# Moving the second context transpose and the self attention's projection behind the PV of step 5

## The chip, the cores and the metric

One core of one Trainium2 chip runs the whole layer. The metric is the device time of one execution in microseconds (us), lower is better. The kernel is written for each engine by hand: TensorE (PE in the profile, PEld for its weight loads), VectorE (DVE), ScalarE (ACT), GpSimd (POOL) and SyncE (SP, which issues the DMAs). Each engine runs its own list of instructions strictly in program order, and semaphores order the engines against each other.

## The reference, cut to what matters

Eight batch entries of 112 tokens by 256 channels go through one decoder layer:

```
x = LN(x + self_attention(x))            # 16 heads of 16, rotary; heads and batch are swapped before the reshape to (8, 112, 256)
x = LN(x + cross_attention(LN'(x), ctx)) # 16 heads of 64, ctx is 375 x 256 per entry
x = LN(x + moe_ffn(x))                   # 8 experts, top 2, and a shared one
```

Only the first two lines are touched. Because of that swap, two heads of the self attention over all batch entries give the rows of one output entry, and the kernel goes through it in that order. For one entry, self attention ends in a projection (256 to 256) whose sum with x is normalised to x1; x1 is normalised again, transposed and projected to the queries of the cross attention. The keys of the cross attention are `ctx @ w_k`, which needs the context transposed, 256 channels on the partitions in two halves of 128.

## The kernel before, in words

All heavy products are split into a high and a low part (three matmuls for one). After a matmul or a transpose into PSUM, ACT copies the high part to SBUF (`..._hi`) and DVE computes the low part (`..._lo`) as the difference, so nearly every PE result passes through ACT and then DVE before PE may use it.

The attention block runs a software pipeline over the entries b = 0 to 7 (`iterations`, L625: b = 0 unrolled, b = 1 to 6 in a loop, b = 7 unrolled). An iteration has eight steps, s = 0 to 7, one for each pair of cross attention heads. In step s PE does, in this order (L1582 and after): `scores` of pair s; `k_project` of pair s + 2 (in steps 6 and 7 those of pairs 0 and 1 of entry b + 1); now and then a value projection; `p_transpose` of pair s - 1 (the probabilities, six transposes); `pv` of pair s - 2. DVE takes the scores' maxima, ACT the exponentials, POOL the reciprocals and the normalisation of the probabilities.

Between these, the self attention of the next entry b + 1 is laid in pieces, called fills. The table `FILL_AT` (L96) says which fill goes to which place of which step: the key is (step, place), and each of PE, ACT and DVE reads the same table through its own function `place(n)` (L1584, L945, L1236). It is thus an order written out by hand; nothing plans it. Places stand at these points of step 5:

- PE: scores(5), k_project(7), place 1, p_transpose(4), place 3, pv(3), place 4.
- ACT: k_hi(7), place 1, the exponentials of pair 5, place 3, `o_hi`(3), `cpt_hi`(4), place 4.
- DVE: `cpt_lo`(3), the maxima of pair 5, k_lo(7), place 1, place 3, `o_lo`(3), place 4.

Step 6 then begins on DVE with `cpt_lo`(4), `x1_moments` (L1091, which normalises with a reciprocal root from POOL), the maxima of pair 6, `xn_norm` and `k_lo` of the next entry's pair 0; on ACT with k_hi and the exponentials of pair 6; on PE with scores(6), `k_project` of the next entry's pair 0, a value projection, p_transpose(5), the fill NT (transposes of xn) and pv(4).

The fills that matter here are those of step 5 for entry b + 1:

- OT: transposes of the self attention's output rows, which come by DMA; `ot_hi` on ACT, `ot_lo` on DVE.
- C0 and C1: the transposes of the two channel halves of the context, three transposes each; `ctx_hi` (L826) on ACT, `ctx_lo` (L1079) on DVE.
- PJ: the projection, six matmuls (`out_project`, L1433), nothing on ACT, and `residual_moments` (L1084) on DVE: the sum `res`, `bn_stats`, `bn_aggr` and a small add that is the input of POOL's reciprocal root.

The waits that tie them:

```
ctx_transpose(b, 1): pe.wait_ge(sg["ot_lo"], b + 1)                  # C1 after ot_lo
free("PJ"):          pe.wait_ge(sg["ctxt_lo"], 2 * b + 1)            # PJ after ctx_lo of C0
k_project(b, p):     pe.wait_ge(sg["ctxt_lo"], 2 * b + 2)            # after ctx_lo of C1
k_project(b, p):     pe.wait_ge(sg["oct_lo"], PAIRS * b + p - 4)     # for p = 0: after o_lo of pair 3 of the entry before
pv(b, s):            cpt_lo of pair s, kt_lo of k_done, oct_lo of pair s - 1
x1_moments(b):       n1_rstd from POOL, which waits for residual_moments
```

SP loads the next context when both context transposes of an entry are done, and the next residual rows when `res` is done. Entry 0's own self attention stands in a prologue with its own order and does not read the table.

Of the kernel before, what the change touches and what calls it, by code (L numbers as in the profile page):

```python
# [94 lines left out]

FILL_AT = {(0, 2): ["QA"], (0, 3): ["QB"], (0, 4): ["KA"], (1, 0): ["KB"], (1, 3): ["S0", "S1"],  # L96
           (2, 1): ["S2", "S3"], (2, 3): ["T0"], (2, 4): ["T1"], (3, 1): ["O0", "T2"],
           (3, 2): ["T3"], (3, 4): ["O1"], (5, 1): ["OT", "C0"], (5, 3): ["C1", "PJ"],
           (6, 3): ["NT"], (7, 1): ["Q0", "Q1"]}

V_AT = {0: "V02", 2: "V10", 3: "V11", 4: "V12", 6: "V00", 7: "V01"}
# [2208 lines left out]
```

## Time and profile before

| | us |
|---|---|
| time, median of 3 runs | 675.41 (675.35 to 676.03) |
| the profiled execution's own time | 675.51 |
| its span, first to last instruction | 673.7 |
| PE busy | 561.5 (83%) |
| DVE busy | 476.8 (71%) |
| ACT busy | 406.5 (60%) |
| POOL busy | 262.9 (39%) |

The span is what the trace shows; the profiled execution's own time is 1.8 us more, for what lies around it, and stands 0.1 us from the median. Busy shares are means over stages with different limits. The attention block lies between about 88 and 490 us of the span. A row of the timeline gives the start and duration of an instruction (or of several merged ones), and in brackets how long its engine had been idle before it and what released it. Two instructions of ACT or DVE in a row overlap a little in the rows: the distance from start to start is then shorter than the duration. That distance is called a slot below.

### The profile page before, as it was taken

Reading aid. Unit: us, or ns where it says so; the run is one execution under the profiler, and the core shown is the slowest. Engines: PE = TensorE matmul, PEld = TensorE weight load, DVE = VectorE, ACT = ScalarE, POOL = GpSimd, SP = SyncE. Lnnn points to the kernel's source line nnn. Section 1 sums busy time; section 2 is a strip of 40 time slices with the busy share of each in tenths; the row PEclk is TensorE's granted clock in tenths of the full one; section 3 lists DMA queues with packets and bytes.
Section 4 is the critical chain, followed back from the end, with each engine's and each line's share of the span. In section 5 each row is a group of like instructions: output and inputs, shape, how many; then the busy total and the mean of one; then the engine's idle time right before and its main releaser. Section 6 shows DMA issues by size and latency. Waiting matters only on the chain. (4 is left out here: it accounts for less than half of the span.)

```text
span 673.7 us, 14735 instructions
## 1 busy us (share of the span) xinstructions
PE 561.5 (83%) x4972; PEld 387.2 (57%) x4972; DVE 476.8 (71%) x921; ACT 406.5 (60%) x979; POOL 262.9 (39%) x292
## 2 busy tenths in 40 slices
PE   5637677799899899899899899989669877999970
PEld 4526345567566567566566566655554644666640
DVE  1985558888888888888888888877668849533333
ACT  2576457487587587587587587565437728534431
POOL 3431034354354354354354354344415822333331
PEclk9975689999999999999999999999857979999995
DMA  8926201311200200200200200401327777333324
GB/s 242 277 70 192 58 18 32 76 32 34 76 32 31 74 31 31 74 31 31 74 31 31 74 31 31 139 32 61 98 70 246 250 213 208 57 63 57 49 32 117
DMA packets 55330, 57.36 MB, mean 85 GB/s; under 512 B 17286, under 2 KB 44238, under 8 KB 55054
## 3 DMA queue, kind: packets, MB, share of 16 engines
q1 hardware_dynamic: 50910, 50.89, 25.3%
q0 software_dynamic: 4384, 5.99, 5.3%
q8 instruction: 22, 0.36, 0.2%
q14 instruction: 14, 0.11, 0.0%
HBM read 46.74 MB, written 10.13 MB: 84 GB/s over the span
## 5 line engine op out<-in xcount | busy, mean ns | idle before, releaser
L728 POOL TENSOR_TENSOR c_rcp<-c_sum,neg_one 112x2 f32<-112x2 f32 x64 | 44.6, 696 | 191.5 <-ACT probs L882 191.5
L732 POOL TENSOR_TENSOR probs<-probs,c_rcp 112x750 f32<-112x750 f32 x64 | 91.8, 1434 | 5.0
L882 ACT ACTIVATE probs<-ps_s,c_neg 112x375 f32<-112x375 f32 x128 | 72.6, 578 | 26.7 <-DVE c_neg L1128 26.6
L766 ACT ACTIVATE kt_hi<-ps_o 128x376 fp32r<-128x376 f32 x64 | 31.8, 497 | 60.3 <-PE ps_o L159 60.3
L1822 POOL DMA_INDIRECT moe_sum<-gsh_hi,xs_in x21 | 33.2, 1583 | 78.7 <-ACT gsh_hi L1870 62.8
L1132 DVE SCALAR_TENSOR_TENSOR cpt_lo<-ps_t,cpt_hi 125x672 f16<-125x672 f32 x64 | 54.3, 849 | 11.7 <-ACT cpt_hi L889 11.7
L1128 DVE TENSOR_REDUCE c_neg<-ps_s 112x2 f32<-112x750 f32 x64 | 59.4, 929 | 1.3 <-PE ps_s L159 1.3
L2102 PE MATMUL ps_h<-w_ex,xst_hi 128*128 (+1 forms) x168 | 58.5, 390 | 0.9 <-DVE xst_lo L1911 0.9
L1507 PE MATMUL ps_t<-ident,probs 112*128 112x112 f32 x384 | 48.3, 262 | 7.6 <-DVE cpt_lo L1132 7.1
L157 PE MATMUL ps_o<-ctxt_hi,w_k_lo 128*128 128x376 f16 x128 | 42.3, 330 | 12.2 <-DVE oct_lo L1141 11.0
L1507 PEld LDWEIGHTS ps_t<-ident,probs 112*128 112x128 f32 x384 | 40.5, 141 | 17.2 <-issue 9.0
L889 ACT ACTIVATE cpt_hi<-ps_t 125x672 f16<-125x672 f32 x64 | 47.5, 742 | 3.3 <-PE ps_o L1524 3.2
L2028 DVE TENSOR_TENSOR gsh_hi<-ps_g,gsh_hi 128x512 f16<-128x512 f32 x21 | 14.5, 690 | 46.9 <-ACT gsh_hi L1864 46.9
L158 PE MATMUL ps_o<-ctxt_lo,w_k_hi 128*128 128x376 f16 x128 | 42.0, 328 | 0.0
L159 PE MATMUL ps_o<-ctxt_hi,w_k_hi 128*128 128x376 f16 x128 | 42.0, 328 | 0.0
L1123 DVE SCALAR_TENSOR_TENSOR v_lo<-ps_vx,v_hi 125x512 f16<-125x512 f32 x48 | 33.0, 688 | 11.4 <-ACT v_hi L874 11.3
L157 PE MATMUL ps_vx<-w_v_hi,ctxt_lo 128*128 128x512 f16 x96 | 37.3, 388 | 2.6 <-DVE res L1147 1.9
L1008 DVE TENSOR_TENSOR kt_lo<-ps_o,kt_hi 128x376 fp32r<-128x376 f32 x64 | 34.7, 542 | 5.0 <-ACT kt_hi L766 5.0
L1847 ACT ACTIVATE s_act<-ps_h,unscale 128x512 f32<-128x512 f32 (+1 forms) x29 | 19.5, 672 | 30.7 <-PE ps_h L2102 30.1
L804 ACT ACTIVATE work<-ps_a,s_neg 112x112 f32<-112x112 f32 x128 | 33.0, 368 | 8.1 <-DVE s_neg L1043 8.1
L874 ACT ACTIVATE v_hi<-ps_vx 125x512 f16<-125x512 f32 x48 | 28.9, 602 | 14.5 <-PE ps_vx L159 14.1
L1524 PE MATMUL ps_o<-cpt_hi,v_lo 125*64 125x112 f16 x384 | 34.7, 222 | 3.5 <-DVE kt_lo L1008 1.7
(337 smaller groups left out, 1755.6 us busy)
## 6 DMA issues: line engine op xcount, KB each, us to landing
chunk<-in_L_ffn_ew_dram SPq DMA_DIRECT2D x24, 512.0 KB, 3.5
spare<-in_L_ffn_ew_dram SPq DMA_DIRECT2D x18, 512.0 KB, 6.2
store<-in_L_ffn_ew_dram SPq DMA_DIRECT2D x6, 512.0 KB, 6.0
ctx_raw<-in_ctx_dram SPq DMA_DIRECT2D x8, 375.0 KB
moe_in<-chunk SPq DMA_DIRECT2D x1, 2709.0 KB, 13.8
plain_raw<-in_L_xattn_w_kv_dram SPq DMA_DIRECT2D x2, 1024.0 KB, 17.1
xs_in<-moe_in SPq DMA_DIRECT2D x15, 129.0 KB, 2.0
ctx_all<-in_ctx_dram SPq DMA_DIRECT2D x1, 1800.0 KB, 22.7
```

Source lines behind the costliest of these rows:

```text
L157: eng.matmul(out, ll, rh, start=start, stop=False, **kw)
L158: eng.matmul(out, lh, rl, start=False, stop=False, **kw)
L159: return eng.matmul(out, lh, rh, start=False, stop=stop, **kw)
L728: pool.tensor_tensor(c_rcp[:, s % 2, :], c_sum[:, s % 2, :], neg_one[:, :], ALU.pow).then_inc(sg["c_rcp_ready"], 1)
L732: pool.tensor_tensor(p, p, r, ALU.mult).then_inc(sg["p_normed"], 1)
L882: act.activation(probs[:, s % 2, h, 0:SK], ps_s[0:N, h, 0:SK], ACT.Exp, bias=c_neg[:, s % 2, h:h + 1], accum_out=c_sum[:, s % 2, h:h + 1]) ...
L889: act.activation(cpt[0][:, :, :, :].rearrange("p h t n -> p h (t n)"), ps_t[0:SKT, :, 0:ST * N], ACT.Copy, scale=P_SCALE).then_inc(sg["cpt ...
L1008: return dve.tensor_tensor(dst, src, part.bitcast(F32), ALU.subtract)
L1128: dve.tensor_reduce(c_neg[:, s % 2, :], ps_s[0:N, :, 0:SK], X, ALU.max, negate=True).then_inc(sg["c_neg_ready"], 1)
L1132: dve.scalar_tensor_tensor(cpt[1][:, :, :, :].rearrange("p h t n -> p h (t n)"), ps_t[0:SKT, :, 0:ST * N], P_SCALE, cpt[0][:, :, :, :].rea ...
L1507: last = pe.transpose(ps_t[:, h, t * N:(t + 1) * N], probs[:, s % 2, h, t * SKT:t * SKT + P], ident[0:N, 0:N])
L2102: last = pe.matmul(out, lhs[a], rhs[b], start=start and n == 0, stop=stop and n == 2)
```

## The change

One entry of the table moves, and since all three engines read the table, it moves on each of them:

```diff
-           (3, 2): ["T3"], (3, 4): ["O1"], (5, 1): ["OT", "C0"], (5, 3): ["C1", "PJ"],
+           (3, 2): ["T3"], (3, 4): ["O1"], (5, 1): ["OT", "C0"], (5, 4): ["C1", "PJ"],
```

The order in step 5 is then:

- PE: ..., OT, C0, p_transpose(4), pv(3), C1, PJ.
- ACT: ..., ctx_hi of C0, the exponentials of pair 5, o_hi(3), cpt_hi(4), ctx_hi of C1.
- DVE: ..., ot_lo, ctx_lo of C0, o_lo(3), ctx_lo of C1, residual_moments.

The programs of POOL and SP are the same, and no instruction or wait is added or taken away. It holds for the iterations b = 0 to 6, seven in all.

## Rows read from the trace of the kernel before

**Rows 1.** Windows: us; PE, PEld, DVE, ACT, POOL busy (x); PEclk; DMA share; GB/s.
```profile
331.47:381.77 50.30, 47.07 (x498) 33.01 (x492) 41.47 (x81) 36.20 (x100) 22.32 (x25) 1.00 0.16 46
```

**Rows 2.** Timeline of PE, steps 4 to 6 (start us, us, what, [idle <-releaser]).
```profile
324.51 0.77 PE L1507 MATMUL ps_t<-ident,probs 112*128 112x112 f32 x6
325.20 0.24 PE L1524 MATMUL ps_o<-cpt_hi,v_lo 125*64 125x112 f16 x2
...
328.48 0.74 PE L1507 MATMUL ps_t<-ident,probs 112*128 112x112 f32 x6
329.46 0.51 PE L1429 MATMUL ps_a<-ident,ctx_raw 125*128 125x125 f32 x3 [0.24 <-DVE ot_lo L1075]
330.08 0.35 PE L157 MATMUL ps_a<-w_proj_hi,ot_lo 128*112 128x256 f32 x1
...
330.95 0.24 PE L1524 MATMUL ps_o<-cpt_hi,v_lo 125*64 125x112 f16 x2
...
331.51 0.44 PE L157 MATMUL ps_s<-kt_hi,qt_lo 64*112 64x376 f32 x2
...
333.05 0.33 PE L157 MATMUL ps_o<-ctxt_hi,w_k_lo 128*128 128x376 f16 x1 [0.76 <-DVE oct_lo L1141]
...
336.24 0.41 PE L1442 MATMUL ps_a<-ident,xn 112*128 112x112 f32 x2 [0.19 <-DVE xn L1028]
```

**Rows 3.** Timeline of ACT, steps 5 and 6.
```profile
330.33 0.58 ACT L833 ACTIVATE ctxt_hi<-ps_a,v_scale 128x375 f16<-128x375 f32 x1
331.62 0.26 ACT L897 ACTIVATE oct_hi<-ps_o 128x112 f16<-128x112 f32 x1 [0.71 <-PE ps_o L1524]
331.78 0.73 ACT L889 ACTIVATE cpt_hi<-ps_t 125x672 f16<-125x672 f32 x1
...
335.90 0.57 ACT L882 ACTIVATE probs<-ps_s,c_neg 112x375 f32<-112x375 f32 x1 [1.12 <-DVE c_neg L1128]
```

**Rows 4.** Timeline of DVE, steps 5 and 6.
```profile
329.37 0.61 DVE L1081 SCALAR_TENSOR_TENSOR ctxt_lo<-ps_a,v_scale,ctxt_hi 128x375 f16<-128x375 f32 x1
330.94 0.61 DVE L1081 SCALAR_TENSOR_TENSOR ctxt_lo<-ps_a,v_scale,ctxt_hi 128x375 f16<-128x375 f32 x1 [0.96 <-ACT ctxt_hi L833]
...
332.66 0.15 DVE L1023 TENSOR_SCALAR mv<-mv 112x1 f32<-112x1 f32 x1
332.73 0.26 DVE L1141 SCALAR_TENSOR_TENSOR oct_lo<-ps_o,oct_hi 128x112 f16<-128x112 f32 x1
332.91 0.85 DVE L1132 SCALAR_TENSOR_TENSOR cpt_lo<-ps_t,cpt_hi 125x672 f16<-125x672 f32 x1
333.68 0.40 DVE L1028 TENSOR_SCALAR x<-res,mv,rstd 112x256 f32<-112x256 f32 x1
...
334.94 0.93 DVE L1128 TENSOR_REDUCE c_neg<-ps_s 112x2 f32<-112x750 f32 x1
...
336.10 0.54 DVE L1008 TENSOR_TENSOR kt_lo<-ps_o,kt_hi 128x376 fp32r<-128x376 f32 x1
337.97 0.28 DVE L1141 SCALAR_TENSOR_TENSOR oct_lo<-ps_o,oct_hi 128x112 f16<-128x112 f32 x1 [1.33 <-ACT oct_hi L897]
```

**Rows 5.** Waits from 81 to 490 us: us in total, times, longest us.
```profile
DVE ctxt_lo L1081 <- ACT ctxt_hi L833: 6.7, 7, 1.0
```

**Rows 6.** Timeline of ACT in step 7: what follows a cpt_hi.
```profile
338.94 0.77 ACT L889 ACTIVATE cpt_hi<-ps_t 125x672 f16<-125x672 f32 x1
339.55 0.54 ACT L766 ACTIVATE kt_hi<-ps_o 128x376 fp32r<-128x376 f32 x1
```

**Rows 7.** Timeline of DVE in the prologue: from the small add, over POOL's root, to x1.
```profile
82.38 0.15 DVE L1023 TENSOR_SCALAR mv<-mv 112x1 f32<-112x1 f32 x1
83.23 0.41 DVE L1028 TENSOR_SCALAR x<-res,mv,rstd 112x256 f32<-112x256 f32 x1 [0.69 <-POOL rstd L721]
```

**Rows 8.** Timeline of PE in iteration 0: a long wait of PE.
```profile
125.85 0.32 PE L157 MATMUL ps_o<-ctxt_hi,w_k_lo 128*128 128x376 f16 x1 [2.05 <-DVE oct_lo L1141]
```

**Rows 9.** Busy time by stretch, around that wait.
```profile
122.70:128.10 5.40, 3.31 (x41) 2.39 (x34) 5.20 (x7) 1.99 (x5) 1.66 (x2) 1.00 0.40 118
```

## The prediction

> **What bounds the kernel now.** I read the page's busy shares first, then the windows of one loop period, then the timeline of each engine around the moved piece, and last the waits. A period is 50.30 us, with PE busy for 47.07 and DVE for 41.47, at a granted clock of 1.00 [rows 1]. So no engine is full, and what ends a stretch is read from the waits. The moved piece lies from 329.2 to 337 us, the passage from step 5 to step 6, and there the load changes hands:
>
> - PE has holes. C1 waits 0.24 us for ot_lo, PJ starts at 330.08, only just after ctx_lo of C0 has ended (329.37 + 0.61 = 329.98), and the key projection at 333.05 waits for oct_lo, the low part of pair 3's output, with 0.76 us idle [rows 2, 4].
> - DVE idles for 0.96 us, until ctx_lo of C1 starts at 330.94 [rows 4]. From there it has no bracket, thus no wait, up to 336.10 + 0.54 = 336.64. What comes out of that run opens the other engines: ACT's exponentials of pair 6 start at 335.90 after 1.12 us of idle, released by DVE's maxima [rows 3]; NT on PE starts at 336.24, released by xn [rows 2]; pv(4) waits by the code for the kt_lo that ends at 336.64; and DVE's next instruction, oct_lo at 337.97, waits over ACT for that pv [rows 4].
>
> So from 330.94 to 336.64 the chain of DVE is what everybody waits for, and its start is set by ctxt_hi on ACT. The iterations are alike: the wait of ctx_lo for ctxt_hi comes 7 times, 6.7 us in all, longest 1.0 [rows 5].
>
> **The change, part by part.** Nothing is added or taken away; three engines get another order, seven times. I carry the rows of this passage forward with their own slots.
>
> PE. p_transpose(4) still starts at 328.48. Behind such a block the pv starts 0.69 later (324.51 to 325.20) [rows 2], so pv(3) starts at 329.17 instead of 330.95. Its inputs have long been there. Its slot is 331.51 - 330.95 = 0.56, so C1 starts at 329.73, later than ot_lo would allow, and its wait of 0.24 is gone. A block of three transposes plus the way to PJ took 330.08 - 329.46 = 0.62 with PJ's wait in it; without one PJ would come sooner, at the earliest at 330.05, which ctx_lo of C0 sets. I take 330.08, as before. PJ's slot is 330.95 - 330.08 = 0.87, and scores(6) starts at 330.95, 0.56 earlier. That is the visible gain on PE.
>
> ACT. The exponentials of pair 5 end their turn at 330.33 [rows 3]. By then pv(3) is through: it took 331.62 - 330.95 = 0.67 from its first matmul to oct_hi, thus 329.84. oct_hi now takes the slot at 330.33 (before 331.62), cpt_hi follows 0.16 later at 330.49, and only behind it, one slot of cpt_hi later, ctxt_hi of C1. Such a slot is 339.55 - 338.94 = 0.61 [rows 6], so ctxt_hi starts at 331.10. Before it started at 330.33: 0.77 later. Its input has been ready since 329.73 + 0.51 = 330.24; what holds it is its place in the queue.
>
> DVE. ctx_lo starts 0.61 behind ctxt_hi (330.33 to 330.94) [rows 3, 4], thus at 331.71, again 0.77 later. DVE has nothing to put there: o_lo(3) runs at about 330.62 for 0.26, and the rest up to 331.71 is idle, since cpt_lo(4), whose input would be ready at 330.49 + 0.73 = 331.22, stands in step 6 behind residual_moments. The run then goes as before, with one instruction fewer in it: ctx_lo, res, the statistics, the small add (332.66 becomes 333.43), then cpt_lo at once. The oct_lo that left the run had a slot of 332.91 - 332.73 = 0.18 [rows 4]. So cpt_lo is late by 0.77 - 0.18 = 0.59, at 333.50, and x1 may start at 333.50 + 0.77 = 334.27. It also needs POOL's root: in the prologue, where DVE only waited for it, x1 came 83.23 - 82.38 = 0.85 after the small add [rows 7], thus 333.43 + 0.85 = 334.28. The later of the two counts: x1 is late by 334.28 - 333.68 = 0.60. Before, oct_lo and cpt_lo together hid the root; now cpt_lo alone just hides it.
>
> The slot of the removed oct_lo is the term with two readings. The rows give 0.18 from start to start, against its 0.26 of duration. The Trainium skill (VectorE: DVE Perf Modes, The DRAIN you can't avoid) says that the next instruction does not start until the pipe has emptied. If its whole duration were freed, cpt_lo would be late by 0.51 only, but x1 still by 0.60, since the root holds it then.
>
> What follows. The maxima of pair 6 move from 334.94 to 335.54, the exponentials from 335.90 to 336.50, xn and NT from 336.24 to 336.84, kt_lo's end from 336.64 to 337.24, all by 0.60. PE's side gains: the key projection waits for oct_lo (now about 330.62 + 0.26 = 330.88) and for ctx_lo of C1 (331.71 + 0.61 = 332.32, plus the 0.06 that PE took behind oct_lo's end, 332.99 to 333.05). It starts at 332.38, 0.67 earlier, with a new releaser. But behind it, the value projection and p_transpose(5), PE comes to NT, which ended a wait of 0.19 and now ends one of 0.19 + 0.67 + 0.60 = 1.46. The gain is given to a wait. p_transpose(5) itself also waits for cpt_lo(4), 333.50 + 0.85 = 334.35; PE comes to it about 334.4, so nothing is added.
>
> Queues. POOL's program is unchanged: the normalisation of pair 5 is long done when the root is asked for at 333.58, and both roots and the next reciprocal come 0.6 late with their inputs. SP issues the next context load after C1, about 0.3 later, and the residual rows after res, 0.77 later; both are first used in the next iteration, whole steps away. The DMAs of the expert weights stand behind these and are taken up by DVE from step 2 on. I cost all of these at nothing; if that cover were gone it would add at most the same few tenths once an iteration.
>
> Sum: all four engines pass 337 us late by 0.60, and each later wait in the period hangs on them, not on a fixed time. 7 x 0.60 = 4.2 us. Made against the profiled execution, 675.51 + 4.2 = 679.7; the median of the runs is 0.1 lower, 679.6. Bounds for one iteration: at the low end, ACT's cpt_hi counted with a short slot of 0.56 and the root at its quickest, 0.50; at the high end, oct_lo's removal gives back nothing, 0.77. That is 3.5 to 5.4, or 678.9 to 680.8.
>
> **The rivals.**
>
> *PE sets the pace (faster).* pv(3) comes 1.78 earlier, oct_lo with it, and the key projection opens at 332.38 instead of 333.05. If what follows hung on PE, each iteration would gain 0.67, 4.7 in all: 670.7. For it: PE is the busiest engine by far and the 0.76 wait behind oct_lo is a clear hole [rows 1, 2]. Against it: the next thing PE feeds into DVE here, the kt_lo at 336.10, had no wait [rows 4]; DVE reached it late, not PE. It decides from the point where DVE's run would start no later than 330.94 + 0.18, and it starts 0.6 past that.
>
> *The delay is absorbed (same).* DVE idles 1.33 before 337.97 [rows 4]; if part of such holes were waits for something that does not move, 0.60 would vanish in them. For it: the holes are larger than the delay. Against it: that one waits for a pv that waits for kt_lo, which moves. Half absorbed gives 677.5, wholly 675.4.
>
> *The clock falls (much slower).* PE's wait of 1.46 before NT is new. In iteration 0 PE stood for 2.05 in one piece at a granted clock of 1.00 for that stretch [rows 8, 9], so this should do nothing. If a tenth of each period ran at the 1.2 GHz level instead of 2.4, PE's 47.07 would grow by 4.7, seven times: 713. The Trainium skill (TensorE: Matmul & The Clock Gate, Part 1) has the gate halve the clock after idling, which speaks against any change that gathers PE's idle time into one piece; the rows just named give it little weight here.
>
> **How the numbers follow.** Forecast 0.82; PE sets the pace 0.07; absorbed 0.09; clock 0.02. What a measurement can tell from no change is 0.2%, 1.35 us. Half of the absorbed case stays within it. So faster 0.07, same 0.06, slower 0.87. The predicted time is 679.6. The range, 677.2 to 681.4, takes in the forecast's bounds and the half absorbed case, and leaves out some 0.16.
>
> **What would show it.** In the changed kernel's timeline: oct_hi directly behind the exponentials of pair 5, cpt_hi, then ctxt_hi some 0.77 later than now against the step's start; DVE with a new idle piece of about 0.8 between oct_lo and ctx_lo; no wait of ctx_lo's successors up to kt_lo; the key projection released by ctxt_lo instead of oct_lo; a wait of about 1.5 of PE before NT; a period of 50.9 instead of 50.3. A period of 49.6 with no wait before NT would make the forecast wrong on PE; an unchanged period with those waits present, wrong on absorption.

## The result and the profile after

The changed kernel takes 679.91 us (median of 5 runs, 678.08 to 682.19) against 676.03 us of before in the same session: ratio 1.0059, 95% interval 1.0039 to 1.0080, slower. Run once more beside before it came to 680.53 against 676.28, ratio 1.0068 (1.0050 to 1.0086). The forecast was 679.6, in a range of 677.2 to 681.4. Before's own median was 0.6 higher here than the 675.41 that the forecast started from, so the difference is the fairer comparison: forecast 4.2 us, measured 3.9 by the medians, 2.6 to 5.4 by the interval.

In one experiment below, split, one of the 8 executions took 2900.27 us, the others 678.70 to 681.23; it is left out of split's median and ratio, and its cause is not known.

The profiled execution took 678.08, with a span of 676.3, only 2.6 us more than before's. Its attention block, from the first maxima to the last, grew by more: from 388.97 us (94.93 to 483.90) to 393.92 (93.99 to 487.91), 4.95 us; what lies before and behind was 0.9 and 1.4 us shorter in this execution. In the second profile of the same kernel the block is 393.74 and the rest behind it 190.76, 1.0 longer than before's 189.80. So the ends scatter by a microsecond or two, and the block is what the change moved.

One period of the loop in the changed kernel (windows: us; PE, PEld, DVE, ACT, POOL busy (x); PEclk; DMA share; GB/s), the answer to [rows 1]:

```profile
334.06:385.03 50.97, 46.87 (x492) 33.03 (x492) 41.61 (x80) 36.13 (x100) 22.36 (x25) 1.00 0.16 45
```

The same work in 50.97 instead of 50.30 us, at an unchanged clock of 1.00: PE and DVE are busy as long as before (46.87 and 41.61 against 47.07 and 41.47), so only waiting was added. The seven periods, from one res to the next, grew by 0.80, 0.79, 0.62, 0.73, 0.59, 0.67 and 0.71 us, 4.9 in all; the first of them, iteration 0, is shorter than the others in both kernels (49.24 and 50.04).

PE in the same passage as [rows 2]. The changed kernel's p_transpose(4) starts at 330.29, before's at 328.48, so 1.81 aligns the two clocks:

```profile
330.29 0.74 PE L1507 MATMUL ps_t<-ident,probs 112*128 112x112 f32 x6
330.96 0.24 PE L1524 MATMUL ps_o<-cpt_hi,v_lo 125*64 125x112 f16 x2
...
331.52 0.54 PE L1429 MATMUL ps_a<-ident,ctx_raw 125*128 125x125 f32 x3
331.89 0.34 PE L157 MATMUL ps_a<-w_proj_hi,ot_lo 128*112 128x256 f32 x1
...
332.75 0.43 PE L157 MATMUL ps_s<-kt_hi,qt_lo 64*112 64x376 f32 x2
...
334.37 0.33 PE L157 MATMUL ps_o<-ctxt_hi,w_k_lo 128*128 128x376 f16 x1 [0.84 <-DVE ctxt_lo L1081]
...
338.72 0.41 PE L1442 MATMUL ps_a<-ident,xn 112*128 112x112 f32 x2 [1.35 <-DVE xn L1028]
```

The wait before C1 is gone and scores(6) comes early. But the key projection is now released by ctxt_lo, and the gain stands before NT as a wait of 1.35 (0.19 before).

ACT, the answer to [rows 3]:

```profile
332.14 0.27 ACT L897 ACTIVATE oct_hi<-ps_o 128x112 f16<-128x112 f32 x1
332.29 0.75 ACT L889 ACTIVATE cpt_hi<-ps_t 125x672 f16<-125x672 f32 x1
332.90 0.60 ACT L833 ACTIVATE ctxt_hi<-ps_a,v_scale 128x375 f16<-128x375 f32 x1
...
338.38 0.57 ACT L882 ACTIVATE probs<-ps_s,c_neg 112x375 f32<-112x375 f32 x1 [2.28 <-DVE c_neg L1128]
```

Three instructions without a bracket: ACT works through its queue, and ctxt_hi, whose input was there since about 332.06 (331.52 + 0.54), comes last. The next exponentials then wait 2.28 us for DVE (1.12 before). DVE, the answer to [rows 4]:

```profile
331.18 0.61 DVE L1081 SCALAR_TENSOR_TENSOR ctxt_lo<-ps_a,v_scale,ctxt_hi 128x375 f16<-128x375 f32 x1
332.44 0.28 DVE L1141 SCALAR_TENSOR_TENSOR oct_lo<-ps_o,oct_hi 128x112 f16<-128x112 f32 x1 [0.65 <-ACT oct_hi L897]
333.53 0.61 DVE L1081 SCALAR_TENSOR_TENSOR ctxt_lo<-ps_a,v_scale,ctxt_hi 128x375 f16<-128x375 f32 x1 [0.82 <-ACT ctxt_hi L833]
...
335.25 0.15 DVE L1023 TENSOR_SCALAR mv<-mv 112x1 f32<-112x1 f32 x1
335.32 0.85 DVE L1132 SCALAR_TENSOR_TENSOR cpt_lo<-ps_t,cpt_hi 125x672 f16<-125x672 f32 x1
336.15 0.41 DVE L1028 TENSOR_SCALAR x<-res,mv,rstd 112x256 f32<-112x256 f32 x1
...
337.42 0.93 DVE L1128 TENSOR_REDUCE c_neg<-ps_s 112x2 f32<-112x750 f32 x1
...
338.58 0.54 DVE L1008 TENSOR_TENSOR kt_lo<-ps_o,kt_hi 128x376 fp32r<-128x376 f32 x1
340.46 0.27 DVE L1141 SCALAR_TENSOR_TENSOR oct_lo<-ps_o,oct_hi 128x112 f16<-128x112 f32 x1 [1.33 <-ACT oct_hi L897]
```

Two holes, 0.65 and 0.82, stand where one of 0.96 stood, and then the same run without a wait. The waits from 81 to 490 us (us in total, times, longest) show that all iterations behave so; the first row also counts the transposes of xn in the prologue, with 1.26:

```profile
PE ps_a L1442 <- DVE xn L1028: 10.9, 8, 1.5
DVE ctxt_lo L1081 <- ACT ctxt_hi L833: 5.7, 7, 0.8
PE ps_o L157 <- DVE ctxt_lo L1081: 5.5, 7, 0.8
```

### The profile page after: what moved, and what is told of

Its sections match the earlier page's. It is cut to its first block and busy times, and to the rows that moved or that the text cites. A ratio compares the mean times of both kernels' runs of the same rounds, so it can differ in the third digit from the quotient of the medians.

```text
span 676.3 us, 14735 instructions
## 1 busy us (share of the span) xinstructions
PE 558.9 (83%) x4972; PEld 385.7 (57%) x4972; DVE 477.8 (71%) x921; ACT 406.5 (60%) x979; POOL 264.6 (39%) x292
## 5 line engine op out<-in xcount | busy, mean ns | idle before, releaser
L874 ACT ACTIVATE v_hi<-ps_vx 125x512 f16<-125x512 f32 x48 | 28.9, 603 | 15.5 <-PE ps_vx L159 15.1
L158 PE MATMUL ps_vx<-w_v_lo,ctxt_hi 128*128 128x512 f16 x96 | 37.6, 392 | 0.0
```

The source lines that it names most:

```text
L158: eng.matmul(out, lh, rl, start=False, stop=False, **kw)
```

## The experiments

All were run beside before, in three sessions on three chips: pe_only, act_dve_only, ctx_first and split in the first, ctx_first_warm, after_warm, cpt_early and split_root in the second, root_only and the changed kernel again in the third. Each was timed 5 to 12 times. The times are medians, the ratio and its 95% interval are against before's runs of the same session (medians 677.00, 676.45 and 676.28). The ratio is not the quotient of the two medians and can stand up to 0.2% from it; differences in us below are worked out from the ratio unless said otherwise. Periods are read from the one profile of each kernel. Below, "clean period" is the distance from one res to the next in the loop's iterations in which the granted clock is 1.00; before's are 50.1 to 50.35, the changed kernel's 50.9 to 51.0.

| kernel | time | ratio (interval) | clean period |
|---|---|---|---|
| changed, again | 680.53 | 1.0068 (1.0050, 1.0086) | 50.9 to 51.0 |
| pe_only | 676.41 | 0.9995 (0.9982, 1.0009) | 50.3 to 50.4 |
| act_dve_only | 692.40 | 1.0229 (1.0207, 1.0251) | 52.2 to 52.3 |
| ctx_first | 679.24 | 1.0025 (1.0004, 1.0047) | 50.25 to 50.4 |
| ctx_first_warm | 675.76 | 1.0002 (0.9988, 1.0016) | 50.2 to 50.3 |
| after_warm | 680.74 | 1.0069 (1.0047, 1.0091) | 50.9 to 51.0 |
| cpt_early | 683.82 | 1.0126 (1.0101, 1.0150) | 51.1 to 51.4 |
| split | 679.51 | 1.0040 (1.0026, 1.0054) | 50.7, once 51.67 |
| split_root | 673.35 | 0.9955 (0.9938, 0.9972) | 50.0 to 50.1 |
| root_only | 676.31 | 1.0000 (0.9986, 1.0014) | 50.3 |

### PE's new order alone

```diff
+FILL_OLD = {**FILL_AT, (5, 3): ["C1", "PJ"], (5, 4): []}
 # ACT and DVE, in place(n):
-                            for f in FILL_AT.get((s, n), ()):
+                            for f in FILL_OLD.get((s, n), ()):
```

> Only PE takes the new order (p_transpose(4), pv(3), C1, PJ); ACT and DVE keep the order of before. Queue theory: what costs in the change is the place of ctxt_hi on ACT behind oct_hi and cpt_hi. Here C1 is ready at 330.24 on the clock of the rows of before, ctxt_hi keeps its 330.33 and ctx_lo its 330.94, so the period stays 50.30 within 0.05 and the time within 0.5 us of before, although scores(6) comes 0.56 earlier. Rival, PE sets the pace: the 0.56 of scores(6) is a gain of up to 3.9 us. Rival, C1 behind pv is itself what costs: about +0.65 an iteration, +4.5 us, as in the changed kernel.

The time did not move. PE in that kernel, and ACT:

```profile
333.98 0.33 PE L159 MATMUL ps_o<-ctxt_hi,w_k_lo 128*128 128x376 f16 x1 [1.34 <-DVE oct_lo L1143]
```

```profile
331.25 0.58 ACT L835 ACTIVATE ctxt_hi<-ps_a,v_scale 128x375 f16<-128x375 f32 x1
331.70 0.28 ACT L899 ACTIVATE oct_hi<-ps_o 128x112 f16<-128x112 f32 x1
```

ctxt_hi keeps its place right behind the exponentials, and what PE won at scores(6) is added to its wait before the key projection, 1.34 instead of 0.76. PE's order neither gains nor costs; the rival that PE sets the pace has fallen, and so has the one that C1 behind pv is itself what costs.

### ACT's and DVE's new order alone

The same edit, on PE's `place` only.

> Only ACT and DVE take the new order; PE keeps C1 and PJ ahead of pv(3). Queue theory: oct_hi waits for pv(3) until 331.62 on the clock of the rows of before, cpt_hi follows at 331.78, ctxt_hi at 332.39, ctx_lo at 333.00 instead of 330.94, less the 0.18 of oct_lo and plus some 0.06 of POOL's root: +1.9 to +2.0 an iteration, 13 to 14 us, time about 689.5. Rival, only PE's order matters: no change. Rival, half absorbed in later holes: +7 us.

```profile
342.72 0.26 ACT L899 ACTIVATE oct_hi<-ps_o 128x112 f16<-128x112 f32 x1 [1.19 <-PE ps_o L1526]
342.88 0.72 ACT L891 ACTIVATE cpt_hi<-ps_t 125x672 f16<-125x672 f32 x1
343.50 0.58 ACT L835 ACTIVATE ctxt_hi<-ps_a,v_scale 128x375 f16<-128x375 f32 x1
```

The clean period is 1.96 to 2.04 above before's, as expected. The time is 15.5 us above (0.0229 x 677.0), some 2 more than expected: three of the periods of the profile, every second one, were 53.3 to 53.5, and in those the granted clock fell to 0.50 for some 3 us, as in the next experiment.

### ctxt_hi of C1 ahead of cpt_hi

```diff
 # ACT, at the end of step s
+                    if s == 5:
+                        place(4)
                     if s >= 1:
                         cpt_hi(b, s - 1)
...
-                    place(4)
+                    if s != 5:
+                        place(4)
```

> The changed kernel with one swap on ACT in step 5: ctxt_hi of C1 ahead of cpt_hi(4) instead of behind it. Queue theory: ctxt_hi comes one oct_hi slot (0.16) later than before the change, ctx_lo at 331.10 on the old clock; oct_lo's 0.18 is out of the run; POOL's root (0.90 from the small add) then holds x1 at +0.05. Period 50.35, time +0.3 us over before (-0.3 to +1.0), so nearly all of the changed kernel's loss of 0.65 an iteration is gone. Rival, the loss comes from DVE's or PE's new order and not from ACT's queue: the time stays at +4 to +5 us.

```profile
331.36 0.27 ACT L897 ACTIVATE oct_hi<-ps_o 128x112 f16<-128x112 f32 x1
331.50 0.59 ACT L833 ACTIVATE ctxt_hi<-ps_a,v_scale 128x375 f16<-128x375 f32 x1
331.96 0.76 ACT L889 ACTIVATE cpt_hi<-ps_t 125x672 f16<-125x672 f32 x1
```

In the clean periods, nearly all of the loss of the changed kernel is gone: 50.25 to 50.4, each 0.07 to 0.14 above the same period of before, where 0.05 was expected. This pins the loss on one slot of cpt_hi ahead of ctxt_hi. But three of the seven periods were 51.3 to 51.5, and the time is 1.7 us above before (0.0025 x 677.0; 2.2 by the medians), more than the expected +1.0 at most. PE's wait before NT is still 1.35 or 1.36 in iterations 1 to 6 (1.48 in iteration 0):

```profile
235.39 0.41 PE L1445 MATMUL ps_a<-ident,xn 112*128 112x112 f32 x2 [1.35 <-DVE xn L1031]
285.80 0.41 PE L1445 MATMUL ps_a<-ident,xn 112*128 112x112 f32 x2 [1.35 <-DVE xn L1031]
```

and behind the second of them the clock falls. Windows of ctx_first, columns as above, the same two stretches of an undisturbed iteration first:

```profile
234.60:237.60 3.00, 1.90 (x27) 1.26 (x28) 1.47 (x4) 2.55 (x9) 1.38 (x3) 1.00 0.03 9
237.60:240.80 3.20, 2.93 (x46) 2.33 (x45) 2.93 (x4) 2.17 (x6) 1.79 (x2) 1.00 0.00 0
285.00:288.00 3.00, 1.88 (x27) 1.25 (x28) 1.48 (x4) 2.54 (x9) 1.38 (x3) 1.00 0.01 4
288.00:291.20 3.20, 3.20 (x24) 2.32 (x23) 2.92 (x4) 2.27 (x6) 1.80 (x2) 0.52 0.00 0
```

In 288.0 to 291.2 the granted clock is 0.52, that is nearly all at 1.2 GHz, and PE gets 24 matmuls started where it started 46. What stands ahead is the same in both iterations, to 0.02 us of PE's busy time. The period with the fall is 51.52, the one without 50.41: 1.1 us for each. The falls in the loop of act_dve_only (three) and of cpt_early below (one) come at the same point, some 2 us behind the transposes of xn, where the wait had been 1.35 to 1.51.

### The wait filled with work

```diff
 # PE, step 6, behind p_transpose(5) and ahead of NT
+                    if more and s == 6:
+                        pe.wait_ge(sg["ctxt_lo"], 2 * (b + 1) + 2)
+                        for _ in range(10):
+                            pe.transpose(bank("NT")[:, 0:P], ident[:, :], ident[:, :])
                     place(3)
```

> The kernel ctx_first, with ten transposes of the identity into the free bank of NT while PE waits for xn in step 6 (1.35 us idle there); they are written over. In ctx_first's profile three of seven periods were 51.3 to 51.5 instead of 50.3 to 50.4, each with the granted clock at 0.50 from some 2.4 us after that wait. Clock theory: with the wait filled the clock stays at 1.00 in the loop, all periods are 50.3 to 50.45, the time is +0.7 us over before (0 to +1.2) and its runs lie within 3 us of each other as before's do, where those of ctx_first lay within 8. Rival, the clock falls for another reason (the wait of POOL, the DMAs): the dips stay, the median stays some 2 us over before. Rival, the transposes hold up NT: +0.1 to +0.3 an iteration, up to +2 us more.

> The changed kernel with the same ten transposes in PE's wait before NT. Queue theory: the loss of 0.65 an iteration has nothing to do with the clock and stays; period 50.95 each, time +4.5 us over before (+4.0 to +5.2). Clock theory on top: the runs of the changed kernel went from 678.1 to 682.2, of before from 675.4 to 676.4; with the wait filled the range falls to some 2 us and its top is lost. Rival, the spread comes from elsewhere (prologue, experts): it stays at 4 us.

With the transposes PE waits 0.22 to 0.25 for xn in iterations 1 to 6 (0.38 in iteration 0), the clock stays at 1.00 from iteration 1 to the end of the loop, and ctx_first_warm equals before: 1.0002. Its 12 runs lie within 2.7 us (674.85 to 677.58), those of ctx_first within 7.9 (675.69 to 683.54). The two were timed in different sessions, each against its own before, and one profile was taken of each; but cpt_early, of the same session as ctx_first_warm and with the wait of 1.35 unfilled, did show a fall in its profile. That the gathered wait of PE brings the clock down is thus shown for ctx_first, with that reserve; why only in some iterations is not.

For the changed kernel the filler gained nothing: 1.0069, against 1.0059 and 1.0068 without it, and its runs scatter by 4.4 us (679.35 to 683.77), where those without it scattered by 4.1. Both profiles without the filler have the clock at 1.00 from iteration 1 to the end of the loop, despite the same wait of 1.35. So its loss of 0.65 to 0.7 an iteration is not the clock's, and the part of the expectation that the filler would narrow the spread was wrong. The clock is not out of the spread altogether: in the profile of after_warm, which is its slowest run, the clock fell two more times in iteration 0 (mean 0.90 against 0.94 in the changed kernel's, 51.32 us against 50.04), ahead of the place that the filler covers. One fall lies behind a wait of 1.44, the other at the end of the very wait of [rows 8], here with the row behind it and the window around it:

```profile
127.39 0.47 PE L157 MATMUL ps_o<-ctxt_hi,w_k_lo 128*128 128x376 f16 x1 [2.05 <-DVE oct_lo L1141]
126.00:131.00 5.00, 3.61 (x19) 2.62 (x21) 3.76 (x6) 1.36 (x4) 0.00 (x0) 0.66 0.45 125
```

### cpt_lo in DVE's idle time

```diff
 # DVE: cpt_lo(b, 4) no longer at the start of step 6, but in step 5 ahead of place(4)
+                    if more and s == 5:
+                        cpt_lo(b, 4)
                     place(4)
```

> The changed kernel with cpt_lo(4) on DVE moved from the start of step 6 into DVE's idle 0.8 us before ctx_lo of C1. This shortens DVE's run by its slot of 0.77 and delays its start by some 0.31 (cpt_lo starts when cpt_hi has ended, about 0.46 before ctxt_hi ends). Theory that DVE's run sets the pace by its busy time: -0.46 an iteration against the changed kernel, -3.2 us, about +1 over before. Theory that POOL's root holds x1 at 0.90 behind the small add, uncovered now: +0.31 an iteration against the changed kernel, period 51.25, time about +6.7 us over before.

```profile
335.18 0.86 DVE L1132 SCALAR_TENSOR_TENSOR cpt_lo<-ps_t,cpt_hi 125x672 f16<-125x672 f32 x1 [0.34 <-ACT cpt_hi L889]
335.95 0.60 DVE L1081 SCALAR_TENSOR_TENSOR ctxt_lo<-ps_a,v_scale,ctxt_hi 128x375 f16<-128x375 f32 x1
...
337.66 0.15 DVE L1023 TENSOR_SCALAR mv<-mv 112x1 f32<-112x1 f32 x1
338.56 0.41 DVE L1028 TENSOR_SCALAR x<-res,mv,rstd 112x256 f32<-112x256 f32 x1 [0.74 <-POOL rstd L721]
```

Filling DVE's hole made it slower, by 0.2 to 0.4 an iteration over the changed kernel: x1 comes 0.90 behind the small add whether cpt_lo stands between them or not, and cpt_lo had been there for nothing. The theory of DVE's busy time has fallen; it is a chain in which POOL's root has a share. The time is 8.5 us above before (7.4 by the medians), where 6.7 was expected; one period of 52.35 with a fall of the clock makes up some of it.

### An earlier place for ctxt_hi

The queue theory says that before, too, would gain if ctxt_hi came earlier. It only can between the two exponentials of pair 5:

```diff
 # ACT: exps(b, s) gets a hook between its two heads; before's FILL_AT
+                    if h == 0 and between:
+                        between()
...
-                        exps(b, s)
+                        exps(b, s, (lambda: place(3)) if s == 5 else None)
...
-                    if s not in (1, 6):
+                    if s not in (1, 5, 6):
                         place(3)
```

> The kernel before, with one move on ACT in step 5: ctxt_hi of C1 stands between the two exponentials of pair 5. Queue theory: C1 is ready at 329.97, ctxt_hi starts at about 330.01 instead of 330.33, ctx_lo at 330.62, and DVE's whole run and the period come 0.32 earlier: period 49.98, time -2.2 us. The second exponential ends at 331.14, still before scores(6) wants it at 331.51. Rival, the DVE run is not what the period hangs on: no change, or slower by the late exponential (up to +0.4 an iteration, +2.8 us).

Wrong in sign: slower by 2.7 us. ctxt_hi did start early, but the chain broke further on. (One of its periods, 51.67, has another cause: a wait of PE of 1.16 for the DMA of the self attention's output rows, ahead of OT.) DVE and POOL of split:

```profile
337.15 0.85 DVE L1134 SCALAR_TENSOR_TENSOR cpt_lo<-ps_t,cpt_hi 125x672 f16<-125x672 f32 x1
338.60 0.41 DVE L1030 TENSOR_SCALAR x<-res,mv,rstd 112x256 f32<-112x256 f32 x1 [0.60 <-POOL rstd L721]
```

```profile
336.55 1.43 POOL L732 TENSOR_TENSOR probs<-probs,c_rcp 112x750 f32<-112x750 f32 x1
337.94 0.56 POOL L721 TENSOR_TENSOR rstd<-mv,const_neg_half 112x1 f32<-112x1 f32 x1
```

The root has no bracket: POOL did not wait for its input, it was still normalising pair 5, whose second exponential the move had pushed back. In before the same two rows of POOL were:

```profile
331.29 1.44 POOL L732 TENSOR_TENSOR probs<-probs,c_rcp 112x750 f32<-112x750 f32 x1
332.89 0.56 POOL L721 TENSOR_TENSOR rstd<-mv,const_neg_half 112x1 f32<-112x1 f32 x1 [0.17 <-DVE mv L1023]
```

There the normalisation ended just 0.16 ahead of the root (331.29 + 1.44 = 332.73). x1 on DVE has no bracket in that profile, so DVE's rows warn of nothing; the short bracket of 0.17 on POOL is all that is seen of the margin. So the root goes first:

```diff
 # POOL, step 5, on top of split
+                    if more and s == 5:
+                        rsqrt(rstd[:, 0:1], mv[:, 0, :], "n1", b + 2)
                     normalise(b, s)
-                    if more and s == 5:
-                        rsqrt(rstd[:, 0:1], mv[:, 0, :], "n1", b + 2)
```

> The kernel split with one more swap, on POOL in step 5: the first reciprocal root stands ahead of the normalisation of pair 5 instead of behind it. In split, ctx_lo did start 0.3 earlier, but x1 then waited for the root 0.60 us, because the root stood behind the normalisation that the later exponential had pushed back. POOL queue theory: without that, x1 follows cpt_lo directly and the period is 50.0 to 50.05, 0.25 to 0.3 under before; time -1.8 us against before (-2.4 to -0.8), and 4.8 us under split. Rival: the normalisation of pair 5, now 0.7 or more later, becomes the wait of p_transpose(5) and of NT behind it; then the period is 50.5 or more and the time +1.5 us or more. Rival: the late exponential is what costs; then nothing changes against split (+3 us over before).

```profile
331.73 0.85 DVE L1134 SCALAR_TENSOR_TENSOR cpt_lo<-ps_t,cpt_hi 125x672 f16<-125x672 f32 x1
332.50 0.40 DVE L1030 TENSOR_SCALAR x<-res,mv,rstd 112x256 f32<-112x256 f32 x1
...
335.07 0.41 DVE L1030 TENSOR_SCALAR xn<-x,mv,rstd 112x256 f32<-112x256 f32 x1 [0.39 <-POOL rstd L721]
```

```profile
331.71 0.56 POOL L721 TENSOR_TENSOR rstd<-mv,const_neg_half 112x1 f32<-112x1 f32 x1 [5.44 <-DVE mv L1025]
...
333.02 1.43 POOL L732 TENSOR_TENSOR probs<-probs,c_rcp 112x750 f32<-112x750 f32 x1
334.41 0.56 POOL L721 TENSOR_TENSOR rstd<-mv,const_neg_half 112x1 f32<-112x1 f32 x1
```

```profile
334.50 0.79 PE L1509 MATMUL ps_t<-ident,probs 112*128 112x112 f32 x6 [0.21 <-POOL probs L732]
```

x1 follows cpt_lo at once, the period is 50.0 to 50.1, and the kernel beats both: 673.35, 3.0 us (1.9 to 4.2) under before. Two waits are new. p_transpose(5) waits 0.21 for the late normalisation. And the second root, which xn needs, now stands behind that normalisation (334.41, no bracket), so xn waits 0.39 and starts 4.78 behind res, where before it was 4.31 (331.47 to 335.78). Neither costs anything that the period shows. The attention block in its profile is 1.6 us shorter than before's (387.37), about what the periods say; the rest of the 3.0 is not placed. The swap by itself is the control:

> The kernel before with POOL's swap alone (the first root of step 6 ahead of the normalisation of pair 5), without the move of ctxt_hi. Theory that the gain of split_root is the earlier start of DVE's run and the swap only makes room for it: nothing is gained here, since the root was not late before (x1 followed cpt_lo at once), and the normalisation now ends some 2.9 us later, about 335.6 on the clock of the rows of before, behind the 335.31 at which p_transpose(5) began: period 50.3 to 50.6, time 0 to +2 us. Rival, the swap itself is the gain: period 50.05, -1.8 to -3 us as in split_root.

It gains nothing (1.0000), so the gain is the earlier ctxt_hi and the swap only makes room for it. Its trace says one thing more:

```profile
336.39 0.41 DVE L1028 TENSOR_SCALAR xn<-x,mv,rstd 112x256 f32<-112x256 f32 x1 [0.39 <-POOL rstd L721]
```

Here too xn comes 4.77 behind res (331.62), 0.46 later than in before, and kt_lo with it, yet the period is the same 50.3. In all three kernels, before, root_only and split_root, the maxima of pair 6 start 3.46 or 3.47 behind res and the projection to the queries, the first use of xn's transposes, 8.23 behind it. So the last part of DVE's run, xn and kt_lo, can come some 0.46 late at no cost; what sets the period stands in the run up to the maxima.

### The changed kernel again

> The changed kernel, unaltered, once more beside before. Queue theory: +0.65 an iteration, 4.6 us in the median, ratio 1.006 to 1.008. Clock theory on top: single runs lie above that by about 1 us for each iteration in which the clock falls behind PE's wait before NT; if the profile catches one, its period is 52.0 instead of 50.95, with the granted clock at 0.50 some 2.4 us behind the wait. Rival, the 4 us between its runs are the ordinary scatter: before's own runs then scatter as much.

The loss came out as expected, 4.6 us (0.0068 x 676.28; 4.25 by the medians). The clock fell nowhere in iterations 1 to 6 of this profile, and before's own 17 runs of the session went from 674.46 to 677.91, wider than the changed kernel's 6 from 679.88 to 682.15. Before's 25 runs of the first session lie 3.7 us apart. So the 4 us between the changed kernel's first runs are about the ordinary scatter.

## Why the prediction was right

- **What bounds.** DVE's run from ctx_lo of C1, started by ctxt_hi's place on ACT. Shown by pe_only (no change of ctxt_hi's place, no change of time), act_dve_only (2.0 an iteration, as carried forward) and ctx_first (0.16 of lateness, about 0.1 left of the loss of 0.7). The prediction took the whole run up to kt_lo for what everybody waits for; root_only shows that its end, xn and kt_lo, has some 0.46 to spare. It made no difference here, since the maxima came late by the same amount.
- **PE.** pv(3), C1, PJ and scores(6) were put at 329.17, 329.73, 330.08 and 330.95; the profile, less 1.81, has 329.15, 329.71, 330.08 and 330.94.
- **ACT and DVE.** ctxt_hi, ctx_lo, the small add and cpt_lo were put at 331.10, 331.71, 333.43 and 333.50; measured 331.09, 331.72, 333.44 and 333.51. oct_lo's slot gave back its 0.18 from start to start and not its 0.26 of duration.
- **POOL's root.** The term that was a little short. It was said to hold x1 at 0.85 behind the small add, as in the prologue [rows 7]; measured 0.90 (335.25 to 336.15), so x1 came 0.66 late instead of 0.60, and the maxima, NT and kt_lo behind it 0.67. Seven times 0.66 is 4.6 us instead of 4.2; the seven periods grew by 4.9, as iterations 0 and 1 lost 0.8 each, which is not explained.
- **The number.** The nearness of 679.6 to 679.91 is partly luck: the forecast was short by 0.4 to 0.7 us in the loop, before's median moved by 0.6, and the changed kernel's 5 runs lie 4.1 apart. What is borne out is a loss of 4 to 5 us, made of seven nearly equal parts.
- **PE's wait before NT.** Forecast 1.46, measured 1.35. The key projection opened 0.23 behind the end of ctx_lo (333.53 + 0.61 = 334.14 to 334.37), not 0.06 as behind oct_lo, and xn came 0.06 later: 1.46 - 0.17 + 0.06 = 1.35. The 0.17 costs nothing, as it eats into a wait.
- **Rivals.** PE sets the pace: fallen with pe_only. Absorbed: fallen for this delay, every period shows the loss, though root_only shows that a delay of xn and kt_lo alone is absorbed. The clock: no fall behind this wait in the changed kernel's two profiles, but given too little thought. The row that was to rule it out, a single wait of 2.05 at full clock [rows 8, 9], rules out nothing: in ctx_first a wait of 1.35 was followed by a fall three times in seven, and in after_warm the same wait of 2.05 ended at a granted clock of 0.50. Its price was put too high: a fall that took a period's mean granted clock to 0.97, thus some 6% of it at half clock, would by the prediction's sum cost 0.06 x 47.07 = 2.8 us and cost 1.1.
- **Queues.** POOL was costed at nothing, rightly for this change. But "long done" was wrong as a picture of before: the normalisation ended 0.16 ahead of the root, and split ran into it.

## What to carry to other kernels

Where each engine takes its queue in order, a move "behind" another piece is a different move on each engine: carry the rows forward engine by engine, and look for the instruction that starts the longest run without waits. An earlier input gains nothing for an instruction that stands later in its queue. Before moving anything past a step, list the ends that just make it, with no bracket behind them or a short one; the rows of the one who waits show waits, not margins. The reverse holds as well: an instruction that others wait for need not set the pace, as xn's 0.39 of new waiting in root_only shows.

## What the runs showed of the hardware

- The granted clock fell from 2.4 to 1.2 GHz behind a wait of PE of only 1.35 us in a loop in which PE is busy for 46.85 of 50.41 us: in three of seven iterations of ctx_first, at 1.1 us each, in three of act_dve_only (waits of 1.35 to 1.51) and in one of cpt_early. In two profiles of the changed kernel the same wait of 1.35 was followed by none. The wait of 2.05 in iteration 0 left the clock at 1.00 in before and ended at 0.50 in after_warm. Ten transposes of the identity in the wait kept the clock up in ctx_first_warm.
- A root of 112 x 1 on POOL costs DVE 0.85 to 0.90 us from the start of the small add to the instruction that uses it, though POOL's own row is 0.56; one DVE instruction with a slot of 0.77 does not quite cover it.
- PE started 0.06 us behind the reported end of oct_lo (0.26 us long), but 0.23 behind that of ctx_lo (0.61 us). The producer's duration is not what decides: in the same trace PE started 0.05 to 0.06 behind pt_lo (0.61) and xnt_lo (0.93). What does was not looked into.
